# Input statistics of tiles 12 to 31: from VectorE's statistics instructions to ScalarE's accumulated sums

## What is computed

```python
def _layernorm(x, eps=1e-05):
    m = mean(x); v = var(x)                 # over the 256 columns
    return (x - m) / sqrt(v + eps)
def fp4_linear(x, w):                       # both sides in blocks of 16, FP4 grid
    return fp4_quant_dequant(x) @ fp4_quant_dequant(w).T
gate, y = fp4_linear(x, w_gate), fp4_linear(x, w_up)      # 256 -> 704
out = fp4_linear(silu(gate) * y, w_down)                  # 704 -> 256
```

## Time and profile before

| | |
|---|---|
| median of 3 runs | 918.5 us (918.35 to 918.93) |
| profiled execution, its own time | 917.84 us |
| its span | 916.0 us |
| granted TensorE clock | 1.00 throughout |
| busy: PE, VectorE (DVE), ScalarE (ACT), GpSimd (POOL) | 888.2, 711.8, 601.6, 528.4 us |
| first FFN, rounds 0 to 31 | about 51 to 264 us of the span |

### The profile page before, as it was taken

One profiled execution on the slowest core, in us unless ns is written; L12 is line 12 of the kernel. 1 busy time (PEld: TensorE's weight loads), 2 busy tenths in 40 slices (PEclk: granted clock), 3 DMA queues, 4 the chain that ended last, 5 costly groups with the idle time before them and its releaser, 6 DMA issues.

```text
span 916.0 us, 16066 instructions
## 1 busy us (share of the span) xinstructions
PE 888.2 (97%) x5608; PEld 796.9 (87%) x5608; DVE 711.8 (78%) x1189; ACT 601.6 (66%) x1263; POOL 528.4 (58%) x562
## 2 busy tenths in 40 slices
PE   4999999999999999999999999999999999999997
PEld 3789889889988898989998898988988899999986
DVE  7979999999976666665573644545599999999998
ACT  6777667767674675758675576767784666555543
POOL 5577778777520254545663154546577667777662
PEclk9999999999999999999999999999999999999999
DMA  9100000000000000000000000000000000000001
GB/s 317 60 1 1 1 1 2 1 1 1 1 2 0 1 2 1 1 1 1 1 1 1 1 1 1 1 1 1 1 1 1 1 25 24 24 24 24 24 1 47
DMA packets 11951, 13.80 MB, mean 15 GB/s; under 512 B 864, under 2 KB 11104, under 8 KB 11872
## 3 DMA queue, kind: packets, MB, share of 16 engines
q1 hardware_dynamic: 11872, 12.79, 4.2%
HBM read 8.59 MB, written 4.19 MB: 14 GB/s over the span
## 4 chain that ended last, share of the span: by engine, by line
PE 64%; DVE 26%; issue 5%; POOL 3%; ACT 1%; DMA 0%; SPq 0%; DVEq 0%; POOLq 0%; ACTq 0%
PE bank L2085 19%; PE bank L1831 12%; PE bank L2123 5%; PE bank L2127 4%; PE bank L2125 4%; DVE amax L787 4%; DVE grid L814 4%; DVE rounded L808 4%; PE bank L1712 4%; DVE z L776 4%; PE bank_b L1842 3%; DVE T_lo L870 3%; PE bank L2048 2%; PE bank_b L1849 2%; POOL p_lo L615 2%
## 5 line engine op out<-in xcount | busy, mean ns | idle before, releaser
L615 POOL TENSOR_TENSOR p_lo<-s_ring,p_hi 128x512 fp32r<-128x512 f32 x128 | 167.4, 1313 | 218.0 <-ACT p_hi L1570 217.9
L982 DVE TENSOR_TENSOR top<-bank,top 128x512 f32<-128x512 f32 x112 | 77.4, 691 | 125.7 <-ACT s_ring L1554 125.7
L1831 PE MATMUL bank<-w_hi,T_hi 128*128 128x512 f32 (+1 forms) x384 | 150.4, 392 | 5.7 <-DVE z L776 5.5
L568 POOL TENSOR_TENSOR zq<-grid,s_neg 128x256 f32<-128x256 f32 (+2 forms) x184 | 141.9, 798 | 17.7 <-DVE grid L814 17.7
L552 POOL TENSOR_TENSOR y<-z,s_inv 128x960 f32<-128x960 f32 (+1 forms) x56 | 98.4, 1757 | 83.8 <-DVE rounded L808 79.0
L1831 PE MATMUL bank<-w_hi,T_lo 128*128 128x512 f32 (+1 forms) x384 | 143.8, 374 | 0.0
L1831 PE MATMUL bank<-w_lo,T_hi 128*128 128x512 f32 (+1 forms) x384 | 143.4, 373 | 0.0
L1382 ACT ACTIVATE T_hi<-bank 128x1024 fp32r<-128x1024 f32 (+1 forms) x68 | 64.6, 951 | 105.1 <-PE bank L1712 105.1
L1554 ACT ACTIVATE s_ring<-bank 128x512 f32<-128x512 f32 x128 | 75.9, 593 | 78.0 <-PE bank L2085 77.9
L2123 PE MATMUL bank<-v_hl,p_hi 128*128 128x258 f32 x384 | 109.9, 286 | 0.4 <-DVE x L1014 0.2
L2127 PE MATMUL bank<-v_hl,p_lo 128*128 128x258 f32 x384 | 108.2, 282 | 0.0
(11 more groups left out here) (232 smaller groups left out, 2204.2 us busy)
## 6 DMA issues: line engine op xcount, KB each, us to landing
out<-x SPq DMA_DIRECT2D x7, 512.0 KB, 2.9
x<-in_L_attn_hidden_states SPq DMA_DIRECT2D x3, 1024.0 KB, 12.3
x<-in_L_attn_hidden_states SPq DMA_DIRECT2D x2, 512.0 KB, 6.9
wraw<-in_L_ffn_w_down SPq DMA_DIRECT2D x1, 704.0 KB, 7.3
wraw<-in_L_ffn_w_up SPq DMA_DIRECT2D x1, 640.0 KB, 4.8
wq_s<-in_L_attn_Wq SPq DMA_DIRECT2D x1, 512.0 KB, 6.4
wk_s<-in_L_attn_Wk SPq DMA_DIRECT2D x1, 512.0 KB, 7.3
wo_s<-in_L_attn_Wo SPq DMA_DIRECT2D x1, 512.0 KB, 8.2
```

What stands on the lines that cost most here:

```text
L568: last = nc.gpsimd.tensor_tensor(out=blocks(zq[:, to:to + hi - lo]), in0=blocks(grid[:, lo:hi]), in1=spread(s_neg[:, par, lo // BLOCK:hi / ...
L615: nc.gpsimd.tensor_tensor(out=lower_buf(n, c), in0=score_buf(n, c), in1=upper_buf(n, c).bitcast(F32), op=ALU.subtract).then_inc(plo_done, 1)
L1831: last = nc.tensor.matmul(gu[:, lo:hi], lhsT=T[:, par, HK + kd, :], rhs=w[:, kd, lo:hi], start=n == 0, stop=n == len(terms) - 1)
```

## The change

ScalarE makes the statistics of tiles 12 to 31, one tile in each of the rounds 0 to 19: `input_sum` behind `mean_of` and ahead of `chain_upper`, `minus_input_mean` (two instructions on 128x1) ahead of `silu_gate`, `input_variance` behind `variance_of` and ahead of `normalise`. VectorE keeps tiles 8 to 11 alone. GpSimd's `group_std` adds eps itself for the groups from 3 on (one more instruction on 128x4) and waits on ScalarE's count of variances in place of VectorE's.

```diff
+        def input_variances(t):
+            return t + 1 if t < 8 else t - 3
...
             def group_std(g):
                 q = slice(4 * g, 4 * g + 4)
-                if g < 2:
-                    pool.wait_ge(x_var, 4 * (g + 1))
+                if g != 2:
+                    pool.wait_ge(x_var, input_variances(4 * g + 3))
                     nc.gpsimd.tensor_tensor(out=var[:, q], in0=var[:, q], in1=eps_all[:, q],
                                             op=ALU.add).then_inc(x_eps, 1)
-                    pool.wait_ge(x_eps, g + 1)
+                    pool.wait_ge(x_eps, g + 1 if g < 2 else g)
                 else:
-                    pool.wait_ge(g_stats, 2 * (g - 1))
+                    pool.wait_ge(g_stats, 2)
...
                 def input_statistics(c):
-                    g = (c + 10) // 4
-                    if c % 4 == 2 and g < NT // 4:
-                        tile_statistics(4 * g)
-                        tile_statistics(4 * g + 1)
-                    if c % 4 == 3 and g < NT // 4:
-                        tile_statistics(4 * g + 2)
-                        tile_statistics(4 * g + 3)
-                        group_statistics(g)
+                    if c == -2:
+                        tile_statistics(8)
+                        tile_statistics(9)
+                    if c == -1:
+                        tile_statistics(10)
+                        tile_statistics(11)
+                        group_statistics(2)
...
                 def step(c, par):
                     blocks_of(c, par)
-                    if f == 0 and c >= 0:
-                        input_statistics(c)
...
+            def input_sum(t):
+                if t % 8 == 0 or t == 12:
+                    act.wait_ge(x_in_s[t // 8 + 1], 16)
+                act.wait_ge(x_var, input_variances(t) - 1)
+                nc.scalar.activation(xjunk[:, 2, :], x[:, t, :], ACT.Identity,
+                                     accum_out=total[:, t:t + 1]).then_inc(x_tot, 1)
+            def minus_input_mean(t):
+                act.wait_ge(x_tot, input_variances(t))
+                nc.scalar.activation(nmean[:, t:t + 1], total[:, t:t + 1], ACT.Copy, scale=-1.0 / D)
+                nc.scalar.activation(nmean_s[:, t:t + 1], total[:, t:t + 1], ACT.Copy,
+                                     scale=-1.0 / D / ROOT).then_inc(x_nm, 1)
+            def input_variance(t):
+                act.wait_ge(x_nm, 2 + t - 11)
+                nc.scalar.activation(xjunk[:, 3, :], x[:, t, :], ACT.Square, scale=1.0 / ROOT,
+                                     bias=nmean_s[:, t:t + 1], accum_out=var[:, t:t + 1]).then_inc(x_var, 1)
...
                     measured = f == 0 and 0 <= c - 2 < NT - 2
+                    arriving = f == 0 and 12 <= c + 12 < NT
...
                         mean_of(c - 2, c - 2)
+                    if arriving:
+                        input_sum(c + 12)
...
                         minus_mean(c - 2, c - 2)
+                    if arriving:
+                        minus_input_mean(c + 12)
...
                         variance_of(c - 2, c - 2)
+                    if arriving:
+                        input_variance(c + 12)
```

## The result

The changed kernel takes **911.5 us** (median of six executions, 911.11 to 911.99) beside 918.85 us for the kernel before (918.35 to 919.99): a ratio of 0.992, interval 0.9908 to 0.9931. The profiled execution took 911.61 us; the one of before took 917.84.

The account below looks back on a forecast made before the run. VectorE, by its statistics, was taken to bound rounds 4 to 19, with PE bounding afterwards. From 917.84 us, 6.47 of PE's waits leave 911.4; the median's 0.66 above gives 912.0 us, range 911.0 to 915.5.

Parts of the forecast that it names:

- the likeliest case: First FFN: PE is the bound in rounds 4 to 19, giving 911.0 to 913.0 us; chance 0.62.
- The gain by PE's waits: Rounds 4 to 19: PE no longer waits for VectorE's `z`, 113.27 us becoming 106.80, a gain of 6.47 us.
- `input_sum` under the wait ahead of `T_hi`: ScalarE, each round: 0.41 to 0.59 us falls into its 1.48 us wait for `T_hi`'s transposes, costing nothing.
- `input_variance` ahead of `normalise`: ScalarE, each round: 0.49 us by issue delays `normalise` and VectorE's `amax`, covered by 0.87 us.
- P: The start of PE's down product in a round, from which the prediction counts times.
- The entry: Rounds 2 and 3: a later `amax` may cost PE one stall, 0.5 + 0.25 us.
- Meetings with the residual: GpSimd's residual holds VectorE's small instructions up to 0.56 us; taken as 0, bounds 0.5 us gain and 4.5 loss.
- What PE allows: Each round: `z` may lag P by 0.97 us before PE waits, with 0.25 us for a restart.
- the rounds after 22: Late first FFN: fewer residual meetings where stalls existed already, taken as 0 with at most 0.5 us gain.
- rival 1: VectorE stays the bound through GpSimd's residual, 2.5 to 4.5 us given back, 914.5 to 916.5 us; chance 0.22.
- The sum: Whole kernel: 917.84 - 6.47 = 911.4 us for a profiled execution, median 0.66 above it, 912.0 us.
- Rival 3: ScalarE's added 1.08 us a round lies on the path through `normalise` to `amax`, up to 929.3 us; chance 0.07.

Follow-up runs that it names:

- The experiment without statistics: Changed kernel with nobody making the statistics of tiles 12 to 31, output not the reference's: 911.31 us.
- the one with both: Kernel before, VectorE keeping all its statistics, with ScalarE also making the same sums and variances where nobody reads them: 919.52 us.
- the one with two groups: Changed kernel with only tiles 12 to 19 on ScalarE, tiles 20 to 31 left with VectorE: 917.65 us.
- The one late round: Changed kernel with two statistics instructions put back on VectorE in round 21 alone, into places nobody reads: 913.09 us.
- scales made from one tensor: `s_up` and `s_neg` made from `amax` and constants in the instruction; on the kernel late once in round 21: 912.23 us, in the best version: 909.03 us.
- `lower` from round 1: Changed kernel with `input_variance` behind `normalise`, and VectorE subtracting for `T_lo` from round 1 on instead of round 4: 909.62 us.

## Why the prediction was right, and where a term was off

The forecast was 912.0 us against 911.5 measured, inside the range, with the likeliest case the one that came. That it lies within 0.5 us is in part luck: 1.0 us of gain that it didn't have is set against 0.32 and 0.1 that it had too much, and the 0.66 us by which the median of before lay above the profiled execution was not there afterwards (911.5 beside 911.61). Point by point:

- **The gain by PE's waits.** 6.47 us were worked out for rounds 4 to 19. The four stretches now take 26.88 + 26.77 + 26.75 + 26.72 = 107.12 us where they took 113.27: 6.15. Of the 0.32 that is missing, 0.15 lie in round 4 (6.83), 0.01 to 0.03 in each of a few others, and 0.08 are PE's pace, 26.72 in place of 26.70 a stretch. The experiment without statistics, the one with both and the one with two groups show together that this is the stalls of VectorE's statistics. (The 9.4 us that the prediction takes from VectorE are the busy time of rows 4, in which instructions overlap, and not the sum of their durations.)
- **`input_sum` under the wait ahead of `T_hi`.** Taken as nothing, and 0.62 us of the wait remain in round 17, 0.6 to 1.1 having been foretold.
- **`input_variance` ahead of `normalise`.** `amax` was put at P + 1.26; with P at 170.12 in round 17 it starts at 171.37, P + 1.25. It waits 0.26 us there, a little over the 0.1 to 0.2 foretold, and `z` of the next round lags its P by 0.10, as foretold.
- **The entry.** It was left open at up to 0.75 us. It cost about 0.15, in round 4, by an `amax` that waited 1.04 us: the experiment with the variance behind the normalisation takes it back. `z` starts 4.32 us behind round 4's first transposes there.
- **Meetings with the residual.** Zero was taken, and all but zero it is in rounds 5 to 19, though the meetings take place: at the end of round 6 `s_up` is held for 0.75 us behind a residual that started at 99.04, and the next `z` starts 0.75 us behind its P (103.97 against 103.22), 0.71 having been worked out. Rounds 7, 8, 11 and 12 lose 0.01 to 0.03 us each. The Trainium skill's rule ("SBUF — State Buffer", Who interferes with whom), the earlier instruction first and the other fully blocked, describes the meeting; the time that would follow if each meeting cost its stall, 914 to 916 us, did not come.
- **What PE allows was a size off.** The prediction let `z` lag P by 0.97 us and put 0.25 for a restart on top of what goes beyond. In rounds 4 to 27 of all fourteen profiles of this study, 336 rounds, one relation holds. Where `z` starts up to 4.18 us behind the first transposes of its round, the round takes 6.67 to 6.69 us; where it starts later, up to 5.9, the next transposes start 2.49 to 2.52 us behind the start of `z`. Two such places, round 4 of the changed kernel and round 7 with the variance twice: `z`, in the first the weight load of PE's next gate product, and the next transposes.

```profile
83.90 0.89 DVE L780 TENSOR_TENSOR z<-bank,silu 128x704 f32<-128x704 f32 x1
84.91 0.19 PEld L1860 LDWEIGHTS bank<-w_hi,T_hi 128*128 128x128 f32 x1
86.41 1.03 PE L1741 MATMUL bank<-ident,zq 128*128 128x128 f32 x8
```

```profile
106.04 0.89 DVE L783 TENSOR_TENSOR z<-bank,silu 128x704 f32<-128x704 f32 x1
108.54 1.03 PE L1750 MATMUL bank<-ident,zq 128*128 128x128 f32 x8
```

P lies 3.46 us behind the first transposes, so `z` may lag by 6.68 - 2.50 - 3.46 = 0.72 us, and what goes beyond costs its own length: the 1.13 of the variance made twice gives 0.41, and 0.42 was lost. The longer first six matmuls (1.64 for 1.39 in the earlier trace rows) are the 0.25 that the 0.97 had too much, and no price on top. The 0.71 worked out for a meeting was thus covered by 0.01 and not by 0.26: that such meetings cost next to nothing is luck.
- **The step that failed: "the rounds after 22".** There the prediction took 0 and allowed 0.5 us. Rounds 24 to 27 took 27.31 us before and take 26.72 now, the last three together 13.80 and 13.37: 0.59 + 0.43 = 1.0 us. These are the four rounds before and after, in the columns of the earlier trace rows:

```profile
218.75:246.06 27.31, 27.31 (x174) 24.78 (x172) 26.58 (x41) 18.43 (x45) 17.40 (x21) 1.00 0.00 1
```

```profile
213.42:240.14 26.72, 26.72 (x173) 24.50 (x172) 25.85 (x39) 18.35 (x45) 17.36 (x21) 1.00 0.00 1
```

PE counts as busy for all of both, but in the chain that ended last VectorE stands alone from 208.86 us on before, and PE alone in the changed kernel. The prediction saw the row, the held `s_neg` of round 23, and read it as a meeting that may or may not come again. It was the start of a loop. VectorE left the statistics late and worked its lag off in rounds 20 to 22, which took 6.67 to 6.69 us. But in round 22 the residual came 5.95 us behind the first transposes, after 6.86 and 6.94 in the two rounds ahead of it, and VectorE was still 0.11 us later there than it is now: the residual started 0.04 us ahead of `s_neg` (211.35 and 211.39), where it now starts 0.07 behind, and from there on it held `s_up` in each round. The one late round put into the changed kernel brings this back, 6.79 to 6.99 us a round, and so shows that lateness alone is enough. The prediction held against rival 1 that PE itself sets the residual's end; in the loop GpSimd's `y` and ScalarE set it, 0.2 us later behind the same down product.
- **The sum.** 6.15 + 1.0 less 0.1 for rounds 0 to 3 makes 7.05 us, and 7.06 is what lies between the first transposes and the last of the first FFN (210.02 against 202.96 us). The medians differ by 7.35. The two profiled executions differ by only 6.23, since round 0 began 0.7 us later in the second, by scatter.
- **Rival 3 had more for it than its 0.07.** It needs 0.87 us more ahead of `amax` by the prediction (0.62 with the 0.72 us that PE allows), but the variance made twice costs 3.1 us with 0.49. The cover had been worked out for each late step alone; a late `amax` and a late residual come from the same instruction and use the same 0.72 us.
- **ScalarE against VectorE.** By the Trainium skill ("ScalarE: Activation LUTs", Rules for kernel authors) elementary arithmetic such as adding and multiplying belongs on VectorE. The busy times agree that it is dearer on ScalarE, by 20.3 against 10.3 us; the time went the other way, since only VectorE was waited for.

Not settled: why scales made from one tensor shorten the second FFN by 0.4 to 0.6 us. In two pairs of kernels they do, but no experiment gives their instructions the old length.

## What to carry to other kernels

Count what the bounding engine waits for, stall by stall, and not the busy time that is removed: here 10.3 us of busy time stood for 7 us, and two fifths of the same move for 1. An engine that runs close behind the bound has one allowance of lag. Read it from many rounds, as the latest start that leaves the round its length, rather than adding it up from single durations (here 0.72 us and not 0.97), and sum into it everything that the same edit delays, on every engine, before calling it covered. Where two engines exclude each other, ask which comes first in a round, as the order may hold until the stage ends (here 0.11 us of lag decided over 1.0); and once another engine is the bound, look for its work that the freed engine can take (`lower` from round 1 brought another 1.35 us).

## What was not expected of the hardware

- A VectorE instruction on 128x60 with one SBUF tensor and two immediates is held by GpSimd's addition on 128x256 as one with two tensors is: 0.76 us where its free twin took 0.18 (199.31 and 199.99 above). The Trainium skill ("SBUF — State Buffer", Who interferes with whom) has `tensor_scalar` among the operations that can take the shared ports, and this row agrees.
- It goes both ways by a few hundredths: GpSimd's addition takes 0.73 us alone, and 0.79 or 0.80 where a small VectorE instruction is issued 0.02 us ahead of it (101.19 and 199.34 above).
- A wait of PE can stay out of the waits that the profile names. In round 4 of the changed kernel none is named, but the weight load of the first gate matmul starts at 84.91, 0.12 us behind the end of `z` (83.90 + 0.89), and the round is 0.15 us longer.
